# A graph network's nodes retiled: 24 tiles of 128 and one of 53 in place of 25 tiles of 125

## The chip, the cores and the metric

The kernel runs on one core of one Trainium2 chip. The metric is the device time of one execution in microseconds, the median of several.

## The reference

There are 3125 nodes with 128 features and 53125 directed edges (with one loop per node), sorted by destination. First comes a graph network of 12 steps on `h = relu(layernorm(x))`, added to x, then two graph convolutions on the layer norm of the sum:

```python
h = tanh(h @ W_in + b_in)
for _ in range(12):
    agg  = segment_sum(h[src], dst) / deg
    diff = tanh(gelu(agg @ W1 + b1) @ W2 + b2)      # 128 -> 256 -> 128
    h    = h + (diff - decay * h) * 0.5
x = x + h
h = relu(layernorm(x))
h = relu(gcn_conv(h, G1, gb1)); x = x + gcn_conv(h, G2, gb2)
# gcn_conv: segment_sum((h @ W)[src] * dinv[src] * dinv[dst], dst) + b, with another loop per node
```

## The kernel before

**Layout.** Nodes lie in 25 tiles (`TILES`) of 125 (`P`): node `k * 125 + p` is row p of tile k. `state` is [125, 25, 128] in float32. The float32 values are split into two float16 parts, `hi` and `lo`, scaled by a power of two. The edges become a dense count matrix `adj` [125 source rows, 25 source tiles, 3125 destinations] in float16, kept in SBUF, so that a sum over edges is a matrix product.

**Edge sums.** `edge_sums` (lines 550 to 569) makes the sums for one of seven groups of destinations, `GROUPS`: six of four tiles (500 columns) and the tail of one (125 columns). For each source tile k it streams `adj[:, k, columns]` twice into one PSUM bank: against the stationary tile `hi[:, k, :]` (L566) and against `lo[:, k, :]` (L567). A turn is all seven groups; there are 12 turns in the loop and 2 in the convolutions. In group 0 TensorE waits for the split of each group of tiles as it comes to it.

**A step.** After the edge sums of group g TensorE makes `outputs(g - 2)` (L587, float32, two passes of 256 hidden rows in halves) and `hidden(g - 1)` (L578, float32, two halves). DVE multiplies by the inverse degrees (`means`, L960), adds the bias (L967), updates the state (L972) and makes `lo` (L800). ScalarE makes gelu (L681), tanh (L689) and `hi` (L637). At the end of a step come `hidden(TAIL)`, `outputs(TAIL - 1)`, `outputs(TAIL)`.

**The start.** SP issues the load of 125 chunk firsts, seven loads of x (L330, one per group), and then the weights, biases and `clearance` (`s_w`, L331 to L342). DVE counts window starts, POOL gathers edges by indirect DMA. DVE waits for `s_w` before its tables (L745 on), makes the first layer norm (L768 to L793), and takes part in the entry product. It then splits each source into tile and row (L842 to L859) while POOL compares destinations (L440, `s_hits`), reduces the hits (L862), and builds one-hot operands (L881) from which TensorE makes `adj` (L505, ScalarE copies it out, L660).

**Degrees.** The norms go out to DRAM and come back, after `adj` is complete, as a row broadcast to 128 partitions (L371) and as a column per node (L374), for DVE at `s_norms_in`. TensorE starts the first step without them.

**Between the loop and the convolutions.** x is loaded again (L393), DVE adds loops to the diagonal of `adj` (L1009, L1012), makes x2 (L1018), statistics and the second split (L1033 to L1037). x2 goes to DRAM (L397) and comes back (L403) under the convolutions. The result is stored in seven DMAs (L410).

A branch for inputs that the windows can't hold (`missed`) isn't taken with these inputs.

Of the kernel before, what the change touches and what calls it, by code (L numbers as in the profile page):

```python
# [20 lines left out]
F32 = mybir.dt.float32  # L21
F16 = mybir.dt.float16
I32 = mybir.dt.int32
ALU = mybir.AluOpType
# [4 lines left out]
P = 125  # L29
TILES = NODES // P  # L30
# [8 lines left out]
GROUPS = [(g * GROUP_TILES, min(GROUP_TILES, TILES - g * GROUP_TILES)) for g in range(7)]  # L39
NG = len(GROUPS)  # L40
TAIL = NG - 1

WIN = 5
WINDOWS = NODES // WIN
WCOLS = WINDOWS // P
SLOTS = 128
CHUNK = EDGES // P
# [11 lines left out]
OPEN = 1  # L59

# [4 lines left out]
def gnn_kernel(nc, x, src, dst, W_in, b_in, W1, b1, W2, b2, clearance, G1, gb1, G2, gb2, out):  # L65
    ctx = ExitStack()
    with ctx:
# [31 lines left out]
        scratch = sb("scratch", [128, 5587], F32)  # L99
# [3 lines left out]
        def col(n):  # L103
# [25 lines left out]
        xload = scratch[0:P, 0:TILES * FEAT].rearrange("p (k f) -> p k f", f=FEAT)  # L129
        o = TILES * FEAT  # L130
        agg = [scratch[:, o:o + 500], scratch[:, o + 500:o + 625]]
        o += 625
        hid = [scratch[:, o:o + 1000].rearrange("p (h n) -> p h n", h=2),
               scratch[:, o + 1000:o + 1250].rearrange("p (h n) -> p h n", h=2)]
        lnt = [scratch[0:P, o:o + 512], scratch[0:P, o + 512:o + 1024]]
        o += 1250
        act_out = scratch[0:P, o:o + 512]
        stats = scratch[0:P, o:o + TILES * 6].rearrange("p (k s) -> p k s", s=6)
        ones_row = scratch[0:1, o - 225:o - 97]
        assert o + 512 == 5587  # L140

        half = scratch[:, :].bitcast(F16)
        nl, nr = 128 * BATCH, P * BATCH
# [10 lines left out]
        assert o <= 5587 * 2  # L154

        yT = [scratch[:, 768 + 500 * i:1268 + 500 * i] for i in range(2)]
        etanh = [scratch[0:P, 1768 + 512 * i:2280 + 512 * i] for i in range(2)]

        o = 0
        e_dst = scratch[0:P, o:o + CHUNK]  # L160
        e_src = scratch[0:P, o + CHUNK:o + 2 * CHUNK]
        o += 2 * CHUNK
        e_sk = scratch[0:P, o:o + CHUNK]
        e_raw = scratch[0:P, o + CHUNK:o + 2 * CHUNK]
        o += 2 * CHUNK
        h = 2 * o
        c625 = half[0:P, h:h + BLOCK]
        h += BLOCK + 1
        gL = half[0:P, h:h + SUB * 128].rearrange("p (c i) -> p c i", c=SUB)
        h += SUB * 128  # L170
        gR = half[0:P, h:h + SUB * BLOCK].rearrange("p (c i) -> p c i", c=SUB)
        h += SUB * BLOCK + 1
        g_one = half[0:P, h:h + 128]
        g_zero = half[0:P, h + 128:h + 256]
        h += 256
        g_rest = half[0:P, h:h + BLOCK]
        h += BLOCK + 1
        g_deg = scratch[0:1, h // 2:h // 2 + BLOCK]
        assert h // 2 + BLOCK <= 5587


        room = adj_flat[:, :].bitcast(F32)
        roomi = adj_flat[:, :].bitcast(I32)
# [23 lines left out]
        wsrc = place(n)  # L207
        quot_i = place(n, roomi)
        quot = place(n)
# [91 lines left out]
        c_use = [sem(f"gcn{n}_rows_ready") for n in range(2)]  # L301
        s_diag = sem("loops_added")
# [6 lines left out]
        x_v = x.rearrange("(k p) f -> p k f", p=P)  # L309
        out_v = out.rearrange("(k p) f -> p k f", p=P)  # L310
        x2_v = x2_dram.rearrange("(k p) f -> p k f", p=P)
# [5 lines left out]
        def window_layout(a):  # L317
            return a.rearrange("(g q d) -> q g d", g=WCOLS, q=P)
# [3 lines left out]
        def _(sp):  # L322
# [24 lines left out]
            with sp.If(missed != 0):  # L347
# [3 lines left out]
                with sp.Fori(0, 5) as j:  # L351
                    with sp.Fori(0, TILES) as k:
# [8 lines left out]
                sp.dma_start(deg[0:P, :].rearrange("p (g d) -> p g d", g=WCOLS), window_layout(deg_dram)  # L361
                             ).then_inc(g_degl, 16)

            sp.wait_ge(s_norms, 1)
            sp.dma_start(window_layout(rdeg_dram), rdeg[0:P, :].rearrange("p (g d) -> p g d", g=WCOLS)
                         ).then_inc(s_norms_out, 16)
            sp.dma_start(window_layout(dinv_dram), dinv[0:P, :].rearrange("p (g d) -> p g d", g=WCOLS)
                         ).then_inc(s_norms_out, 16)
            sp.wait_ge(s_norms_out, 32)
            sp.wait_ge(s_last[2], 1)  # L370
            sp.dma_start(row, rdeg_dram.rearrange("(a n) -> a n", a=1).broadcast_to((128, NODES))  # L371
                         ).then_inc(s_norms_in, 16)
            with nc.allow_non_contiguous_dma("a column of one float per node"):
                sp.dma_start(dinv_col[0:P, :], dinv_dram.rearrange("(k p) -> p k", p=P)).then_inc(s_norms_in, 16)  # L374


            def stream_rest(turn, g):
                k0, nt = GROUPS[g]
                with sp.Fori(0, TILES) as k:
                    sp.wait_ge(s_restu, (turn * NG + g) * TILES + k + OPEN)  # L380
                    sp.dma_start(rest_tile[:, 0:nt * P],
                                 rest_dram[bass.ds(k, 1), :, k0 * P:(k0 + nt) * P].rearrange("k p d -> p (k d)")
                                 ).then_inc(s_rest[g], 16)
# [7 lines left out]
            for g in range(NG):  # L391
                k0, nt = GROUPS[g]
                sp.dma_start(xload[:, k0:k0 + nt, :], x_v[:, k0:k0 + nt, :]).then_inc(s_xr[g], 16)  # L393
# [3 lines left out]
            sp.dma_start(x2_v, state[:, :, :]).then_inc(s_x2o, 16)  # L397
# [3 lines left out]
            sp.wait_ge(s_x2o, 16)  # L401
            sp.wait_ge(c_lo[1], NG)
            sp.dma_start(state[:, :, :], x2_v).then_inc(s_x2i, 16)  # L403
# [3 lines left out]
            for g in range(NG):  # L407
                k0, nt = GROUPS[g]
# [720 lines left out]
```

## Time and profile before

| | us |
|---|---|
| median of 3 runs | 1447.96 (1447.82 to 1449.18) |
| profiled execution | 1448.8 |
| its span, first to last instruction | 1447.0 |
| TensorE busy | 1305.8 (90%) |
| DVE busy | 427.1 (30%) |
| ScalarE busy | 311.8 (22%) |
| mean granted TensorE clock | 0.977 |

Busy times overlap between engines, and a matmul's recorded duration includes its way through the array, so the distance from start to start is its cost in a stream. L with a number is a line of the kernel above; SPq is SP's instruction queue, PEld the weight loads.

### The profile page before, as it was taken

Reading aid. Unit: us, or ns where it says so; the run is one execution under the profiler, and the core shown is the slowest. Engines: PE = TensorE matmul, PEld = TensorE weight load, DVE = VectorE, ACT = ScalarE, POOL = GpSimd, SP = SyncE. Lnnn points to the kernel's source line nnn. Section 1 sums busy time; section 2 is a strip of 40 time slices with the busy share of each in tenths; the row PEclk is TensorE's granted clock in tenths of the full one; section 3 lists DMA queues with packets and bytes.
Section 4 is the critical chain, followed back from the end, with each engine's and each line's share of the span. In section 5 each row is a group of like instructions: output and inputs, shape, how many; then the busy total and the mean of one; then the engine's idle time right before and its main releaser. Section 6 shows DMA issues by size and latency. Waiting matters only on the chain.

```text
span 1447.0 us, 17636 instructions
## 1 busy us (share of the span) xinstructions
PE 1305.8 (90%) x7256; PEld 731.2 (51%) x7256; DVE 427.1 (30%) x802; ACT 311.8 (22%) x429; POOL 31.5 (2%) x31
## 2 busy tenths in 40 slices
PE   0348899999999999999999999999999999849898
PEld 0337745546455554555545555455554555515444
DVE  1999911301213022131121312113121131382312
ACT  0238821301212012121121212112121131300100
POOL 2320000000000000000000000000000000000000
PEclk9969999999999999999999999999999999969999
DMA  3000020000000000000000000000000000130021
GB/s 94 19 0 0 0 46 1 1 0 0 0 0 0 0 0 0 0 0 0 0 0 0 0 0 0 0 0 0 0 0 0 0 0 0 32 102 1 9 51 31
DMA packets 23951, 13.93 MB, mean 10 GB/s; under 512 B 6358, under 2 KB 23326, under 8 KB 23676
## 3 DMA queue, kind: packets, MB, share of 16 engines
q1 hardware_dynamic: 22332, 11.96, 3.2%
q0 software_dynamic: 1600, 1.72, 0.5%
q8 instruction: 12, 0.20, 0.1%
q14 instruction: 7, 0.06, 0.0%
HBM read 10.43 MB, written 3.23 MB: 9 GB/s over the span
## 4 chain that ended last, share of the span: by engine, by line
PE 82%; DVE 10%; issue 4%; SPq 2%; ACT 1%; DMA 0%; DVEq 0%; ACTq 0%
PE ps L566 32%; PE ps L567 32%; PE ps L587 9%; PE ps L578 8%; DVE scratch L881 3%; SPq L330 1%; ACT scratch L681 1%; PE ps L612 1%; DVE scratch L768 1%; DVE ps L967 1%; DVE state L793 1%; DVE lo L800 0%; DVE scratch L1033 0%; PE ps L476 0%; DMA cols<-in_L_gnn_clearance_dram 0%
## 5 line engine op out<-in xcount | busy, mean ns | idle before, releaser
L566 PE MATMUL ps<-adj,hi 125*128 125x500 f16 (+1 forms) x2450 | 828.4, 353 | 29.9 <-DVE lo L1037 25.3
L567 PE MATMUL ps<-adj,lo 125*128 125x500 f16 (+1 forms) x2450 | 827.0, 352 | 0.0
L566 PEld LDWEIGHTS ps<-adj,hi 125*128 125x128 f16 x2450 | 237.6, 97 | 281.8 <-issue 43.7
L567 PEld LDWEIGHTS ps<-adj,lo 125*128 125x128 f16 x2450 | 238.3, 97 | 253.2 <-issue 22.4
L967 DVE TENSOR_TENSOR ps<-ps,bias 125x512 f32<-125x512 f32 (+1 forms) x84 | 53.8, 640 | 561.6 <-PE ps L587 561.6
L689 ACT ACTIVATE scratch<-ps 125x512 f32<-125x512 f32 (+1 forms) x84 | 46.3, 552 | 669.3 <-DVE ps L967 669.3
L578 PE MATMUL ps<-scratch,w 128*128 128x500 f32 (+1 forms) x336 | 141.1, 542 | 13.7 <-ACT scratch L681 13.7
L681 ACT ACTIVATE scratch<-ps,b1c,cols 128x500 f32<-128x500 f32 (+1 forms) x168 | 113.5, 723 | 156.8 <-PE ps L578 156.0
L587 PEld LDWEIGHTS ps<-w,scratch 128*125 128x125 f32 x1200 | 140.5, 188 | 6.6
L587 PE MATMUL ps<-w,scratch 128*125 128x128 f32 x1200 | 143.5, 273 | 0.0
L960 DVE TENSOR_TENSOR scratch<-ps,scratch 128x500 f32<-128x500 f32 (+1 forms) x84 | 52.0, 619 | 188.7 <-PE ps L578 129.9
L505 PE MATMUL ps<-scratch 128*128 128x125 f16 x625 | 81.7, 297 | 16.1 <-DVE scratch L881 15.9
L881 DVE TENSOR_TENSOR scratch<-scratch 128x1536 f16<-128x1536 f16 (+1 forms) x106 | 93.0, 937 | 1.7 <-DVE scratch L870 0.4
L660 ACT ACTIVATE adj<-ps 125x1500 f32 x52 | 77.3, 1486 | 38.6 <-PE ps L505 38.6
L578 PEld LDWEIGHTS ps<-scratch,w 128*128 128x128 f32 x336 | 56.3, 190 | 58.0 <-issue 33.0
L505 PEld LDWEIGHTS ps<-scratch 128*128 128x128 f16 x625 | 66.7, 120 | 30.8 <-DVE scratch L881 30.7
L972 DVE SCALAR_TENSOR_TENSOR state<-state,cols,scratch 125x512 f32<-125x512 f32 (+1 forms) x84 | 58.4, 696 | 58.6 <-ACT scratch L689 58.6
L800 DVE SCALAR_TENSOR_TENSOR lo<-state,cols,hi 125x512 f16<-125x512 f32 (+1 forms) x91 | 58.7, 690 | 33.7 <-ACT hi L637 33.7
L637 ACT ACTIVATE hi<-state,cols 125x512 f16<-125x512 f32 (+1 forms) x91 | 55.8, 666 | 0.1
L467 PE MATMUL ps<-ident,state 125*128 125x125 f32 x25 | 5.0, 340 | 43.8 <-DVE state L793 43.8
L1048 DVE TENSOR_TENSOR scratch<-ps,scratch 128x500 f32<-128x500 f32 (+1 forms) x14 | 8.7, 623 | 105.3 <-PE ps L612 94.1
L467 PEld LDWEIGHTS ps<-ident,state 125*128 125x128 f32 x25 | 3.9, 179 | 43.9 <-issue 43.9
(115 smaller groups left out, 228.0 us busy)
## 6 DMA issues: line engine op xcount, KB each, us to landing
scratch<-rdeg_scratch SPq DMA_DIRECT2D x1, 1562.5 KB
scratch<-dinv_scratch SPq DMA_DIRECT2D x1, 1562.5 KB, 6.7
x_scratch<-state SPq DMA_DIRECT2D x1, 1562.5 KB
state<-x_scratch SPq DMA_DIRECT2D x1, 1562.5 KB
state<-in_x_dram SPq DMA_DIRECT2D x6, 250.0 KB
scratch<-in_x_dram SPq DMA_DIRECT2D x6, 250.0 KB
out_dram<-state SPq DMA_DIRECT2D x6, 250.0 KB
w<-in_L_gnn_W_dram SPq DMA_DIRECT2D x2, 128.0 KB
```

The lines of the kernel that those rows point to most:

```text
L505: return nc.tensor.matmul(target[:, :, place * WIN:(place + 1) * WIN], Lb[buf][:, b, :, i_], Rb[buf][:, b, :, i_].rearrange("p (k d) -> p ...
L566: nc.tensor.matmul(bank, hi[:, k, :], adj[:, k, c0:c0 + n], start=(k == 0), stop=False)
L567: mm = nc.tensor.matmul(bank, lo[:, k, :], adj[:, k, c0:c0 + n], start=False, stop=(k == TILES - 1))
L578: nc.tensor.matmul(ps_hid[h][:, 0:n], w1[:, h * FEAT:(h + 1) * FEAT], agg[g == TAIL][:, 0:n], start=True, stop=True).then_inc(s_hid, 1)
L587: mm = nc.tensor.matmul(ps_out[g == TAIL][0:P, i * FEAT:(i + 1) * FEAT], hid[g == TAIL][:, h, i * P:(i + 1) * P], w2[:, h, :], start=(h == ...
L637: nc.scalar.activation(tiles_of(hi, group), tiles_of(state, group), ACT.Copy, scale=factor).then_inc(s_hi, 1)
L660: nc.scalar.activation(adj[:, :, bass.ds((i * 2 + u) * BATCH * WIN, BATCH * WIN)].rearrange("p k (b c) -> p b k c", b=BANKS), ps[0:P, 3 * ...
L681: nc.scalar.activation(hid[g == TAIL][:, h, 0:n], ps_hid[h][:, 0:n], ACT.Gelu, bias=b1c[:, h:h + 1], scale=now_unscale).then_inc(s_gelu, 1)
L800: V.scalar_tensor_tensor(out=tiles_of(lo, group), in0=tiles_of(state, group), scalar=factor, in1=tiles_of(hi, group), op0=ALU.mult, op1=AL ...
L881: last_ = V.tensor_tensor(buf[:, 0:b, :, 0:w], c_.broadcast_to((128, b, m, w)), k_.broadcast_to((128, b, m, w)), ALU.is_equal)
L967: V.tensor_tensor(p_, p_, bias_of(1, nt), ALU.add).then_inc(s_bias, 1)
L972: V.scalar_tensor_tensor(out=tiles_of(state, g), in0=tiles_of(state, g), scalar=keep[0:P, :], in1=act_out[:, 0:n_], op0=ALU.mult, op1=ALU. ...
```

## The change

Tiles have 128 rows, so 3125 nodes are 24 full tiles (`FULL`) and one of 53 (`SHORT`, tile 24). Its `hi` is in rows 0 to 63 of the stationary tile and its `lo` in rows 64 to 127 (`STACK`), padded with zeros; the rows of `adj` for that tile are copied by a DMA from partitions 0 to 63 to 64 to 127 (`s_pair`). One matmul per group serves both parts. The groups cover 512 columns five times, then 437 (tiles 21 to 23 and the short one), then 128 (tile 20, the tail). Source tiles are taken in `K_ORDER`: 0 to 19, 21 to 23, 24, 20, and in group 0 there is a wait in front of each.

```diff
-P = 125
-TILES = NODES // P
+P = 128
+FULL = NODES // P
+LAST = NODES - FULL * P
+TILES = FULL + 1
+SHORT = TILES - 1
+STACK = 64
...
+GROUPS = [(0, 4), (4, 4), (8, 4), (12, 4), (16, 4), (21, 4), (20, 1)]
+SPANS = [(k0 * P, min(nt * P, NODES - k0 * P)) for k0, nt in GROUPS]
+K_ORDER = [(k, g) for g, (k0, nt) in enumerate(GROUPS[:TAIL]) for k in range(k0, k0 + nt) if k != SHORT]
+K_ORDER += [(SHORT, TAIL - 1), (GROUPS[TAIL][0], TAIL)]
...
             def edge_sums(turn, g, split, first):
-                k0, nt = GROUPS[g]
-                c0, n = k0 * P, nt * P
+                c0, n = SPANS[g]
...
-                for k in range(TILES):
-                    if g == 0 and k % GROUP_TILES == 0:
-                        pe.wait_ge(split, first + k // GROUP_TILES + 1)
+                for at, (k, owner) in enumerate(K_ORDER):
+                    if g == 0:
+                        pe.wait_ge(split, first + owner + 1)
+                        if k == SHORT:
+                            pe.wait_ge(s_pair, 16)
...
+                    nc.tensor.matmul(bank, hi[:, k, :], adj[:, k, c0:c0 + n], start=(at == 0), stop=False)
+                    if k != SHORT:
+                        mm = nc.tensor.matmul(bank, lo[:, k, :], adj[:, k, c0:c0 + n], start=False,
+                                              stop=(k == K_ORDER[-1][0]))
```

`hidden`, `gelu`, `means` and `scaled` take their columns from `SPANS`; `outputs`, `tanh`, bias and update work on whole tiles (512 columns in group 5, cleared once beyond 437). The split on DVE writes the short tile's `lo` with an instruction of its own, in the loop, in the second layer norm and before the second convolution:

```diff
+            def lo_of(group, values, factor):
+                k0, nt = GROUPS[group]
+                k1 = min(k0 + nt, FULL)
+                if k1 < k0 + nt:
+                    V.scalar_tensor_tensor(out=hi[STACK:P, SHORT, :], in0=values[0:STACK, SHORT, :],
+                                           scalar=factor[0:STACK, :],
+                                           in1=hi[0:STACK, SHORT, :], op0=ALU.mult, op1=ALU.subtract)
+                return V.scalar_tensor_tensor(out=lo[:, k0:k1, :], in0=values[:, k0:k1, :], scalar=factor,
+                                              in1=hi[:, k0:k1, :], op0=ALU.mult, op1=ALU.subtract)
```

Loads and stores of nodes go through `rows`, which gives a group's full tiles as one DMA and the 53 rows as another, so eight DMAs for all nodes. Store and reload of x2, single DMAs before, go the same way. The loads of x wait for a POOL memset of the short tile, POOL's first instruction:

```diff
+        def rows(t, dram, g):
+            k0, nt = GROUPS[g]
+            k1 = min(k0 + nt, FULL)
+            pairs = [(t[:, k0:k1, :], dram[k0 * P:k1 * P, :].rearrange("(k p) f -> p k f", p=P))]
+            if k0 + nt == TILES:
+                pairs.append((t[0:LAST, SHORT, :], dram[FULL * P:NODES, :]))
+            return pairs
...
+            sp.wait_ge(s_pad, 1)
             for g in range(NG):
-                k0, nt = GROUPS[g]
-                sp.dma_start(state[:, k0:k0 + nt, :], x_v[:, k0:k0 + nt, :]).then_inc(s_x[g], 16)
+                for sbuf, dram in rows(state, x, g):
+                    sp.dma_start(sbuf, dram).then_inc(s_x[g], 16)
...
             sp.wait_ge(s_last[2], 1)
+            sp.dma_start(adj[STACK:P, SHORT, :], adj[0:STACK, SHORT, :]).then_inc(s_pair, 16)
             sp.dma_start(row, rdeg_dram.rearrange("(a n) -> a n", a=1).broadcast_to((128, NODES))
                          ).then_inc(s_norms_in, 16)
...
-                sp.dma_start(dinv_col[0:P, :], dinv_dram.rearrange("(k p) -> p k", p=P)).then_inc(s_norms_in, 16)
+                sp.dma_start(dinv_col[:, 0:FULL], dinv_dram[0:FULL * P].rearrange("(k p) -> p k", p=P)
+                             ).then_inc(s_norms_in, 16)
+                sp.dma_start(dinv_col[0:LAST, SHORT:TILES], dinv_dram[FULL * P:NODES].rearrange("(k p) -> p k", p=LAST)
+                             ).then_inc(s_norms_in, 16)
```

Windows of edges keep their layout (125 windows a column). The split of a source into tile and row is now two integer operations; fourteen DVE instructions become eight, and the copy ahead of `s_wd` is gone:

```diff
-            V.tensor_copy(wsrc, wsrc_i.rearrange(flat))
             V.tensor_tensor(wdst, wdst_i, base, ALU.subtract).then_inc(s_wd, 1)
-            dve.wait_ge(s_wd, 1)
+            e_ = wsrc_i.rearrange(flat)
+            V.tensor_scalar(rem_i, e_, P - 1, None, ALU.bitwise_and)
+            link(V.tensor_scalar(quot_i, e_, 7, None, ALU.logical_shift_right))
```

Also added: on DVE a second corner of the diagonal, a piece of x2 and two memsets before the loop; on POOL two small memsets.

## Rows read from the trace of the kernel before

**Rows 1.** The page: busy time, chain by engine, and a group of weight loads.
```profile
PE 1305.8 (90%) x7256; PEld 731.2 (51%) x7256; DVE 427.1 (30%) x802; ACT 311.8 (22%) x429; POOL 31.5 (2%) x31
...
PE 82%; DVE 10%; issue 4%; SPq 2%; ACT 1%; DMA 0%; DVEq 0%; ACTq 0%
...
L566 PEld LDWEIGHTS ps<-adj,hi 125*128 125x128 f16 x2450 | 237.6, 97 | 281.8 <-issue 43.7
```

**Rows 2.** Timeline of the last groups: start us, duration us, engine, line.
```profile
1424.64 0.37 PE L567 MATMUL ps<-adj,lo 125*128 125x500 f16 x1
...
1434.80 0.37 PE L567 MATMUL ps<-adj,lo 125*128 125x500 f16 x1
...
1435.88 0.22 PE L566 MATMUL ps<-adj,hi 125*128 125x125 f16 x1
...
1437.99 0.22 PE L566 MATMUL ps<-adj,hi 125*128 125x125 f16 x1
```

**Rows 3.** The chain of waits in step 11: start us, us, what.
```profile
1157.42 1.75 PE ps L587 x16
1159.17 1.68 PE ps L578 x4
```

**Rows 4.** Timeline from the end of step 11 into step 12.
```profile
1166.76 1.42 ACT L681 ACTIVATE scratch<-ps,b1c,cols 128x500 f32<-128x500 f32 x2
...
1168.24 0.71 PE L578 MATMUL ps<-scratch,w 128*128 128x125 f32 x4 [1.14 <-ACT scratch L681]
...
1168.76 0.80 ACT L681 ACTIVATE scratch<-ps,b1c,cols 128x125 f32<-128x125 f32 x2 [0.58 <-PE ps L578]
...
1172.58 0.38 PE L567 MATMUL ps<-adj,lo 125*128 125x500 f16 x1
...
1172.79 0.37 PE L566 MATMUL ps<-adj,hi 125*128 125x500 f16 x1
...
1176.95 1.01 DVE L800 SCALAR_TENSOR_TENSOR lo<-state,cols,hi 125x512 f16<-125x512 f32 x2 [0.26 <-ACT hi L637]
```

**Rows 5.** Timeline of the start, SP's queue, POOL and DVE.
```profile
1.29 19.88 SPq L330 DMA_DIRECT2D state<-in_x_dram  x7
...
12.41 1.21 POOL L429 DMA_INDIRECT adj<-in_dst_dram,adj  x1 [0.30 <-issue]
21.22 0.83 SPq L331 DMA_DIRECT2D w_in<-in_L_gnn_W_in_dram  x1
...
31.77 0.15 DVE L745 TENSOR_SCALAR cols<-cols 128x1 f32<-128x1 f32 x1 [25.95 <-DMA cols<-in_L_gnn_clearance_dram]
```

**Rows 6.** Windows: length, busy by engine, clock granted, DMA share, GB/s.
```profile
21.40:22.40 1.00, 0.00 (x0) 0.00 (x0) 0.00 (x0) 0.00 (x0) 0.00 (x0) 1.00 0.38 95
...
23.40:24.40 1.00, 0.00 (x0) 0.00 (x0) 0.00 (x0) 0.00 (x0) 0.00 (x0) 1.00 0.97 255
...
186.00:196.00 10.00, 8.36 (x32) 3.55 (x33) 0.32 (x1) 2.81 (x4) 0.00 (x0) 0.83 0.11 3
...
200.00:202.00 2.00, 2.00 (x11) 0.87 (x9) 0.00 (x0) 0.00 (x0) 0.00 (x0) 1.00 0.99 404
```

**Rows 7.** Timeline of the window keys, DVE and POOL.
```profile
71.67 0.48 DVE L842 CAST adj<-adj 125x640 f32<-125x640 int32 x1
...
72.98 10.31 POOL L440 TENSOR_SCALAR adj<-adj 125x640 f32<-125x640 f32 x5 [18.07 <-DVE adj L843]
...
83.56 3.47 DVE L862 TENSOR_REDUCE cols<-adj 125x25 f32<-125x3200 f32 x1
```

**Rows 8.** Timeline of the first step's start.
```profile
187.64 0.37 PE L566 MATMUL ps<-adj,hi 125*128 125x500 f16 x1 [2.05 <-ACT adj L666]
...
196.25 0.35 SPq L371 DMA_DIRECT2D scratch<-rdeg_scratch  x1
```

**Rows 9.** Who waited for whom: total us, times, longest.
```profile
PE ps L566 <- DVE lo L1037: 25.3, 3, 24.6
```

**Rows 10.** The same for SP's queue.
```profile
SPq L67 <- DMA out_dram<-state: 4.3, 1, 4.3
```

More of the change, by code:

```diff
@@ L59 @@
 OPEN = 1
+SCRATCH = TILES * FEAT + 512 + 128 + 1024 + 256 + 512
 SPLIT_TOP = 14
@@ L301, in gnn_kernel @@
         c_use = [sem(f"gcn{n}_rows_ready") for n in range(2)]
+        s_pad = sem("short_tile_cleared")
+        s_pair = sem("short_tile_paired")
+        g_pair = sem("general_rest_paired")
         s_diag = sem("loops_added")
@@ L308, in gnn_kernel, with parts @@
         block = ctx.enter_context(nc.Block())
-        x_v = x.rearrange("(k p) f -> p k f", p=P)
-        out_v = out.rearrange("(k p) f -> p k f", p=P)
-        x2_v = x2_dram.rearrange("(k p) f -> p k f", p=P)
+        def rows(t, dram, g):
[5 more added lines that the diff above has]
+            return pairs
+        def parts(g):
+            return 2 if sum(GROUPS[g]) == TILES else 1
         def tiles_of(t, g):
@@ L391, in _ @@
             for g in range(NG):
-                k0, nt = GROUPS[g]
-                sp.dma_start(xload[:, k0:k0 + nt, :], x_v[:, k0:k0 + nt, :]).then_inc(s_xr[g], 16)
+                for sbuf, dram in rows(xload, x, g):
+                    sp.dma_start(sbuf, dram).then_inc(s_xr[g], 16)
             sp.wait_ge(s_x2, NG)
@@ L396, in _ @@
                          ).then_inc(s_dinv, 16)
-            sp.dma_start(x2_v, state[:, :, :]).then_inc(s_x2o, 16)
+            for g in range(NG):
+                for sbuf, dram in rows(state, x2_dram, g):
+                    sp.dma_start(dram, sbuf).then_inc(s_x2o, 16)
             with sp.If(missed != 0):
@@ L400, in _ @@
                     stream_rest(STEPS, g)
-            sp.wait_ge(s_x2o, 16)
+            sp.wait_ge(s_x2o, 16 * (NG + 1))
             sp.wait_ge(c_lo[1], NG)
-            sp.dma_start(state[:, :, :], x2_v).then_inc(s_x2i, 16)
+            for g in range(NG):
+                for sbuf, dram in rows(state, x2_dram, g):
+                    sp.dma_start(sbuf, dram).then_inc(s_x2i, 16)
             with sp.If(missed != 0):
@@ L407, in _ @@
             for g in range(NG):
-                k0, nt = GROUPS[g]
                 sp.wait_ge(c_use[1], g + 1)
-                sp.dma_start(out_v[:, k0:k0 + nt, :], state[:, k0:k0 + nt, :]).then_inc(s_res, 16)
-            sp.wait_ge(s_res, 16 * NG)
+                for sbuf, dram in rows(state, out, g):
+                    sp.dma_start(dram, sbuf).then_inc(s_res, 16)
+            sp.wait_ge(s_res, 16 * (NG + 1))
         @block.gpsimd
@@ L760, in _, with statistics @@
             V.tensor_scalar(unscale, pow2, 2.0**-SPLIT_TOP * DT, None, ALU.mult).then_inc(s_tab, 1)
-            mv = mean_var[0:P, :].rearrange("p (k s) -> p k s", s=2)
-            def statistics(rows):
-                for k in range(TILES):
-                    if k % GROUP_TILES == 0:
-                        rows(k // GROUP_TILES)
-                    last = V.bn_stats(stats[:, k, :], state[:, k, :])
+            mv = mean_var[:, :].rearrange("p (k s) -> p k s", s=2)
+            def statistics(ready):
+                for g, (k0, nt) in enumerate(GROUPS):
+                    ready(g)
+                    for k in range(k0, k0 + nt):
+                        last = V.bn_stats(stats[:, k, :], state[:, k, :])
                 link(last)
@@ L853, in _ @@
[L853 removed]
+            V.tensor_scalar(rem, rem_i, 1.0, None, ALU.add)
             V.tensor_scalar(over, w_, 0.0, None, ALU.is_ge)
[L856 removed]
+            link(V.scalar_tensor_tensor(out=keyf, in0=quot_i, scalar=float(WIN), in1=w_, op0=ALU.mult, op1=ALU.add))
             link(V.scalar_tensor_tensor(out=inside, in0=w_, scalar=float(WIN), in1=over, op0=ALU.is_lt, op1=ALU.mult))
[L858 removed]
@@ L1048, in scaled @@
                     V.tensor_tensor(agg[g == TAIL][:, 0:n_], ps_agg[2 if g == TAIL else g % 2][:, 0:n_],
-                                    row[:, k0 * P:k0 * P + n_], ALU.mult).then_inc(c_aggT[layer], 1)
+                                    row[:, c0:c0 + n_], ALU.mult).then_inc(c_aggT[layer], 1)
                 def rows_out(g):
```

273 lines of the change are left out of this document (139 added, 134 removed).

## The prediction

> **What bounds the kernel now.** I read the page first, then the chain of waits, then the timeline of three places: one step of the loop, the start, and the end. Timeline durations of matmuls overlap, so I take a matmul's cost from the distance between starts.
>
> The page says TensorE is busy 90% of the span, and 82% of the chain that ended last runs through it [rows 1]. So inside the loop a saved TensorE cycle is a saved cycle. What else lies on the chain is a short list: DVE 10%, which is mostly the start, SP's queue 2%, and ScalarE 1%.
>
> The unit of work is `edge_sums`. Its matmuls of 500 columns start every 211.7 ns (from 1424.64 to 1434.80 us, 48 steps) and those of 125 columns every 55.5 ns (from 1435.88 to 1437.99, 38 steps) [rows 2]. That gives 0.4165 ns for a column and 3.4 ns for the instruction. The pace is set by columns streamed, not by weight loads: a load of 97 ns [rows 1] goes by unseen even behind matmuls 55.5 ns apart.
>
> At the end of a step there is one real stall: TensorE waits 1.14 us for the gelu of group 5 before it may write the tail's hidden product [rows 4]. The splits `hi` and `lo` for the next step arrive in time.
>
> The start is another matter. DVE sits until 31.77 us for the last of the weights, and that load is last because SP's queue spends 19.88 us, from 1.29 us on, on issuing seven loads of x [rows 5]. While only these run, the DMA engines are 0.38 busy and move 95 GB/s. Two microseconds later, with the 128-partition weight loads, they are 0.97 busy and move 255 GB/s [rows 6]. So the 125-partition loads use a part of the engines only, and the queue backs up into SP. After that DVE's own chain runs without a pause to 83.56 us, and everything behind it shifts with it.
>
> **The change, part by part.** The working is against the span of 1447.0 us. The profiled execution took 1448.8, 0.8 above the median of 1447.96, so I take the sum off the median.
>
> *Edge sums.* A turn was 50 matmuls in each of seven groups: 50 x (6 x 211.7 + 55.5) ns = 66.3 us. Now it is 49 matmuls, five groups of 512 columns, one of 437, one of 128. By the line above these cost 216.7, 185.4 and 56.7 ns, so 49 x (5 x 216.7 + 185.4 + 56.7) ns = 65.0 us. There are 14 turns (12 steps, 2 layers): 14 x 1.33 = 18.7 us saved. Columns in all are the same 3125; what is saved is one pass in fifty. Bounds: 18 (columns alone) to 19.5.
>
> *Hidden products.* Four matmuls of 500 columns take 1.68 us [rows 3], 0.84 ns a column each. Twelve more columns in five groups cost 4 x 12 x 0.84 x 5 = 0.20 us a step, 2.4 us in 12. Group 5 falls to 437 columns, but its saving of 0.21 us only lengthens the stall behind it. What shortens that stall is the gelu: 1.42 us for two of 500 columns against 0.80 for two of 125 [rows 4] is 0.83 ns a column, so 2 x 63 x 0.83 = 0.10 us a step, 1.3 us in 12. Net +1.1 us. The `outputs` and `product` matmuls keep their count and their 128 moving columns. Their stationaries widen from 125 to 128, at most 2.4% of the 1.75 us of sixteen [rows 3], under 0.05 us a group, 3 to 4 us if all of it showed. I take nothing, because the pace fits two passes of 128 moving columns (107 ns) plus the 3.4, and I keep 0 to 4 for the range.
>
> *The waits of group 0.* They were seven a turn and are 26 (one for each tile, and `s_pair`). A wait that is already met shows no price: the matmul at 1172.79 is the ninth of its group, has such a wait in front, and starts 0.21 us after its neighbour, like any other [rows 4]. I take 0; the dear end is under the rivals. Are they met? `lo` of group 5 and the tail is done at 1177.96, 6.9 us into a group that started at 1171.10 (1172.79 less eight spacings). Its first user is the 41st matmul, at 8.7 us. The extra DVE instruction on the short tile's `lo` (about 0.3 us) is covered by that margin. The tail's tile is now last in order, which only helps.
>
> *The loads of x.* Now 24 tiles go from 128 partitions, and 53 rows in a DMA of their own, behind a short POOL memset (`s_pad`). SP issues the 1562 KB row broadcast, 128 partitions wide, in 0.35 us [rows 8]. Eight such issues are 2.8 us in place of 19.9. The rest of the chain, from 21.22 to 31.77, is 10.6 us, so the weights could be in at 1.3 + 2.8 + 10.6 = 14.7. The traffic doesn't allow quite that: the transfers up to 31.8 us are some 3.4 MB (summed over windows like those of [rows 6]), 13.3 us at the best rate seen with 512-byte rows, 255 GB/s, after a start at about 2.5. POOL's indirect loads share the engines, and the 53 rows may sit on few of them. I take 17 us for the end of DVE's wait, a gain of 14.8. Bounds: no gain if the loads pace as before, 17.1 at 14.7. What comes next is not late: the gathered chunk rows that DVE needs 4.4 us later have been asked for by POOL at 13.6 us [rows 5].
>
> The Trainium skill, "DMA: Bandwidth & Descriptors", section "Why a DMA increments its semaphore by 16 and not by 1", says a DMA from SP runs on the largest number of engines up to 16 that divides its outermost dimensions: 5 for 125 rows, 16 for 128, 1 for 53. The trace agrees in kind: 0.38 of sixteen busy is near five and their bookkeeping. By it alone the x loads would shrink from 625 to 192 packets an engine (245 on the one that has the 53 rows), some 8 us at the pace of the rows, and the sum would be the one I use.
>
> *Window keys.* Six of DVE's fourteen operations from 71.67 us [rows 7] go, 4 to 5 us of work. But POOL's five compares run from 72.98 for 10.31 us, to 83.3, and DVE needs them next [rows 7]. So only the copy that stood ahead of `s_wd` counts, 0.5 us. If POOL ran faster beside an idle DVE it could be up to 4.
>
> *The copy of the short tile (`s_pair`).* It is a DMA of 64 rows, issued where the row broadcast is now, at 196.25, 8.6 us after the first edge matmul at 187.64 [rows 8]. Its user is the 47th matmul: 46 x 0.217 = 10.0 us, plus about 1.6 for the stretch at the lower clock (0.83 granted on average over 186 to 196 [rows 6]), 11.6 us. It moves 0.4 MB; at the 404 GB/s of large rows [rows 6] that is 1 us, and it has some 3 us. I take a stall of 0.3 us, bounds 0 to 2. The row broadcast behind it is late by 1 us. DVE needs it only for `means(0)`, and TensorE that only after group 1.
>
> *Second layer norm, stores.* TensorE waits 24.6 us there for the first `lo` [rows 9], a chain of DVE work. Added: one piece of `x2`, one corner of the diagonal, one piece of `lo`: +0.3 us. The x reload, the store of `x2` and its reload lie under DVE or edge sums and get shorter. At the very end SP waits 4.3 us for the last store [rows 10], which queues behind group 5's. That shrinks with more engines, while the 53 rows add some 1.7 us on theirs: 1.2 us saved, bounds 0 to 2.
>
> Sum: -18.7 + 1.1 + 0 - 14.8 - 0.5 + 0.3 + 0.3 - 1.2 = -33.5. 1448.0 - 33.5 = 1414.5.
>
> **The rivals.**
> *The x loads are no faster.* If 512-byte rows are what costs and not their spread, SP is blocked as before. For it: all x loads have them. Against it: the weights at 23.4 us are mostly 512-byte rows too and fill the engines [rows 6]. Time: 1414.5 + 14.8 + 1.2 = 1430.5.
>
> *They are faster, but the start is bound elsewhere*, by the gathers or by a single engine that has the 53 rows and its share of everything. Then half the gain comes: about 1422.
>
> *The waits cost (the other side).* If a wait in front of each tile keeps the next weight load from being fetched early, its 97 ns [rows 1] come into the open. 19 more waits in 14 turns are 266; at 97 ns they cost 25.8 us, giving 1440. From 126 ns each (33.5 / 266) they eat the whole gain and the kernel gets slower. Against it: the wait at 1172.79 costs nothing.
>
> *The saved matmul saves nothing*, since wider moving operands cost more than the line says. The line has two points, 125 and 500, and 512 is next to the second: hardly possible. It would leave about 1433.
>
> **How the numbers follow.** Forecast 0.71; loads no faster 0.11; start bound elsewhere 0.10; waits cost 0.06 (of which 0.04 slower than before and 0.01 the same); no saving by the matmul 0.02. The likeliest case alone is 1409 to 1420 (upper bound of the loads' gain, POOL's speed-up in part; stationaries, pair stall and clock on the other side). The range takes in the two cases behind it: 1409 to 1431. A difference within 0.2% (2.9 us) is about what a measurement of this kernel can't tell from none; only a wait price near 126 ns lands there. Faster 0.95, same 0.01, slower 0.04.
>
> **What the profile after should show.** SP's x issues short, and DVE's first wait over near 17 us. A step shorter by 1.24 us (18.7 / 14 less 1.1 / 12), matmuls of 512 columns 216.7 ns apart, and no gap between the tiles of group 0. POOL's compares ended last before DVE's reduction. `s_pair` met within a microsecond. The second layer norm's gap stays near 25 us. The prediction is wrong if the first wait ends after 25 us, or if group 0's matmuls are further apart than group 1's.

## The result and the profile after

The changed kernel takes 1422.22 us, the median of 4 runs (1421.82 to 1422.75), against 1447.89 (1447.57 to 1449.18) for the kernel before, in the same session. The ratio is 0.9821, with a 95% interval of 0.9804 to 0.9838. The forecast was 1414.5 with a range of 1409 to 1431: the direction and the range hold, and the time is 7.7 us above the forecast. The profiled execution took 1421.82 us, its span 1420.0.

First the page of the changed kernel, the lines that answer to [rows 1]: instructions, busy time of each engine, and the matmuls of the fp16 product.

```profile
span 1420.0 us, 17490 instructions
...
PE 1289.5 (91%) x7158; PEld 727.4 (51%) x7158; DVE 426.4 (30%) x815; ACT 311.5 (22%) x429; POOL 31.6 (2%) x34
...
L600 PEld LDWEIGHTS ps<-adj,hi 128*128 128x128 f16 x2450 | 238.3, 97 | 281.8 <-issue 47.4
L602 PEld LDWEIGHTS ps<-adj,lo 128*128 128x128 f16 x2352 | 229.4, 98 | 243.6 <-issue 23.5
```

There are 98 fewer matmuls (14 turns of seven groups, one each), and the `lo` line has 2352 where the `hi` line has 2450: that is the shared tile. A weight load still takes 97 ns. TensorE's busy time fell by 16.3 us and the span by 27.0, so more than a third of the gain is not in the matmuls. The page's chain for this execution covers only some 12% of the span, so I compare the two kernels by landmarks, the starts of one instruction that both have.

The start of the changed kernel, in the timeline view (start us, duration us, engine, line, then in brackets the idle time before and what ended it), answers to [rows 5].

```profile
1.31 4.59 SPq L350 DMA_DIRECT2D state<-in_x_dram  x8
...
5.94 0.43 SPq L351 DMA_DIRECT2D w_in<-in_L_gnn_W_in_dram  x1
...
11.42 1.95 SPq L362 DMA_DIRECT2D cols<-in_L_gnn_clearance_dram  x1
12.55 1.21 POOL L462 DMA_INDIRECT adj<-in_dst_dram,adj  x1 [0.30 <-issue]
20.24 0.15 DVE L780 TENSOR_SCALAR cols<-cols 128x1 f32<-128x1 f32 x1 [14.27 <-DMA cols<-in_L_gnn_clearance_dram]
```

SP is through with eight loads of x in 4.59 us where seven took 19.88, and DVE starts at 20.24 instead of 31.77. But the first weight is issued 15.3 us earlier (5.94 against 21.22) and DVE starts only 11.5 us earlier: what remains of the wait is the time from the last issue (11.42) to its landing.

The window keys and the first step of the changed kernel, same view, answer to [rows 7, 8].

```profile
61.13 10.09 POOL L473 TENSOR_SCALAR adj<-adj 125x640 f32<-125x640 f32 x5 [17.75 <-DVE adj L886]
71.25 3.48 DVE L899 TENSOR_REDUCE cols<-adj 125x25 f32<-125x3200 f32 x1 [4.08 <-POOL adj L473]
...
175.31 0.59 PE L600 MATMUL ps<-adj,hi 128*128 128x512 f16 x1 [2.06 <-ACT adj L701]
...
183.95 0.53 SPq L393 DMA_DIRECT2D adj<-adj  x1
184.52 0.58 SPq L394 DMA_DIRECT2D scratch<-rdeg_scratch  x1
...
186.49 5.53 SPq L399 DMA_DIRECT2D cols<-dinv_scratch  x1
188.04 0.90 PE L600 MATMUL ps<-adj,hi 128*128 128x512 f16 x2 [1.19 <-DMA adj<-adj]
```

DVE now has nothing to do before POOL's compares end, and waits 4.08 us for them. The copy of the short tile is issued 8.64 us after the first edge matmul, as in the forecast, but it holds TensorE up by 1.19 us.

One step of the loop is the distance between two loads of ScalarE's table, from the timeline of ScalarE. Step 2 and step 12 of the changed kernel:

```profile
274.35 1.28 ACT L716 ACT_TABLE_LOAD   x1 [1.67 <-DVE cols L1022]
...
1156.01 1.28 ACT L716 ACT_TABLE_LOAD   x1 [1.67 <-DVE cols L1022]
```

and of the kernel before:

```profile
286.13 1.28 ACT L681 ACT_TABLE_LOAD   x1 [1.45 <-DVE cols L983]
...
1178.65 1.28 ACT L681 ACT_TABLE_LOAD   x1 [1.45 <-DVE cols L983]
```

Ten steps took 892.52 us and take 881.66: 89.25 and 88.17 us a step, 1.09 saved where the forecast had 1.24.

Who waited for whom in the changed kernel (total us, times, longest) answers to [rows 9, 10], and to the stall in [rows 4].

```profile
PE ps L600 <- DVE lo L1089: 25.1, 1, 25.1
...
PE ps L613 <- ACT scratch L716: 14.9, 12, 1.2
...
SPq L77 <- DMA out_dram<-state: 2.7, 1, 2.7
```

The wait at the second layer norm grew from 24.6 to 25.1, the stall for the gelu from 1.14 to 1.24 a step, and the last store is waited for 2.7 us instead of 4.3.

### The profile page after: what moved, and what is told of

Read it like the earlier page. It is cut to its first block and busy times, and to the rows that moved or that the text cites. A ratio compares the mean times of both kernels' runs of the same rounds, so it can differ in the third digit from the quotient of the medians.

```text
span 1420.0 us, 17490 instructions
## 1 busy us (share of the span) xinstructions
PE 1289.5 (91%) x7158; PEld 727.4 (51%) x7158; DVE 426.4 (30%) x815; ACT 311.5 (22%) x429; POOL 31.6 (2%) x34
## 5 line engine op out<-in xcount | busy, mean ns | idle before, releaser
L600 PE MATMUL ps<-adj,hi 128*128 128x512 f16 (+2 forms) x2450 | 815.4, 353 | 31.1 <-DVE lo L1089 25.1
L602 PE MATMUL ps<-adj,lo 128*128 128x512 f16 (+2 forms) x2352 | 796.7, 353 | 0.0
L600 PEld LDWEIGHTS ps<-adj,hi 128*128 128x128 f16 x2450 | 238.3, 97 | 281.8 <-issue 47.4
L602 PEld LDWEIGHTS ps<-adj,lo 128*128 128x128 f16 x2352 | 229.4, 98 | 243.6 <-issue 23.5
L613 PE MATMUL ps<-scratch,w 128*128 128x512 f32 (+2 forms) x336 | 141.0, 542 | 14.9 <-ACT scratch L716 14.9
L716 ACT ACTIVATE scratch<-ps,b1c,cols 128x512 f32<-128x512 f32 (+2 forms) x168 | 113.2, 721 | 156.8 <-PE ps L613 155.8
L622 PEld LDWEIGHTS ps<-w,scratch 128*128 128x128 f32 x1200 | 143.3, 192 | 6.3
L622 PE MATMUL ps<-w,scratch 128*128 128x128 f32 x1200 | 146.1, 275 | 0.0
L695 ACT ACTIVATE adj<-ps 128x1500 f32 x52 | 77.3, 1486 | 38.0 <-PE ps L538 38.0
L840 DVE SCALAR_TENSOR_TENSOR lo<-state,cols,hi 128x512 f16<-128x512 f32 (+2 forms) x98 | 61.2, 671 | 30.6 <-ACT hi L672 29.5
```

Of the source, the lines that this page charges most:

```text
L600: nc.tensor.matmul(bank, hi[:, k, :], adj[:, k, c0:c0 + n], start=(at == 0), stop=False)
L602: mm = nc.tensor.matmul(bank, lo[:, k, :], adj[:, k, c0:c0 + n], start=False, stop=(k == K_ORDER[-1][0]))
L613: nc.tensor.matmul(ps_hid[h][:, 0:n], w1[:, h * FEAT:(h + 1) * FEAT], agg[g == TAIL][:, 0:n], start=True, stop=True).then_inc(s_hid, 1)
L622: mm = nc.tensor.matmul(ps_out[g == TAIL][:, i * FEAT:(i + 1) * FEAT], hid[g == TAIL][:, h, i * P:(i + 1) * P], w2[:, h, :], start=(h == 0 ...
L695: nc.scalar.activation(adj[:, :, bass.ds((i * 2 + u) * BATCH * WIN, BATCH * WIN)].rearrange("p k (b c) -> p b k c", b=BANKS), ps[:, 3 * u: ...
L716: nc.scalar.activation(hid[g == TAIL][:, h, 0:n], ps_hid[h][:, 0:n], ACT.Gelu, bias=b1c[:, h:h + 1], scale=now_unscale).then_inc(s_gelu, 1)
```

## The experiments

Every kernel below is the changed kernel with the one edit shown ("..." marks lines left out). The ratio is against the kernel before, run on the same chip beside it; a distance in us from "the changed kernel" is from its 1422.22, measured in another session. The kernel before took 1447.89, 1447.81, 1447.08 and 1449.07 us in the four sessions, so a distance of 1 or 2 us between two medians isn't evidence by itself, and for such small effects I go by landmarks inside the traces.

**Is it the width of the x loads?** The eight loads stay where they are, and each full one is cut at partition 125.

```diff
-                    sp.dma_start(sbuf, dram).then_inc(s_x[g], 16)
+                    if sbuf.shape[0] == LAST:
+                        sp.dma_start(sbuf, dram).then_inc(s_x[g], 16)
+                    else:
+                        sp.dma_start(sbuf[0:125], dram[0:125]).then_inc(s_x[g], 16)
+                        sp.dma_start(sbuf[125:128], dram[125:128]).then_inc(s_x[g], 16)
```

(DVE's wait for x counts one more DMA per group.)

> Only the six wide loads of x at the start are cut in two, partitions 0 to 124 and 125 to 127. Theory (the width of 125 is what confined the loads to a part of the DMA engines): SP's issues of x take 15 to 20 us again, DVE's first wait ends near 30 us and the time is 1431 to 1436, 9 to 14 above the changed kernel's 1422. Rival (the loads got faster because tiles or order differ, or for the larger loads behind them): the first wait stays near 20 us and the time at 1422 to 1424.

Measured: 1433.37 us (1432.65 to 1434.47), ratio 0.9903 [0.9886, 0.9919], 11.2 us more than the changed kernel. Its timeline of SP and DVE at the start:

```profile
2.31 0.28 SPq L353 DMA_DIRECT2D state<-in_x_dram  x1
2.63 2.92 SPq L354 DMA_DIRECT2D state<-in_x_dram  x1
...
22.16 0.37 SPq L355 DMA_DIRECT2D w_in<-in_L_gnn_W_in_dram  x1
...
31.07 0.15 DVE L784 TENSOR_SCALAR cols<-cols 128x1 f32<-128x1 f32 x1 [25.10 <-DMA cols<-in_L_gnn_clearance_dram]
```

and its window of 6 to 8 us (length, busy by engine, granted clock, DMA share, GB/s), then the same window of the changed kernel:

```profile
6.00:8.00 2.00, 0.00 (x0) 0.00 (x0) 0.00 (x0) 0.00 (x0) 1.40 (x1) 1.00 0.38 95
```

```profile
6.00:8.00 2.00, 0.00 (x0) 0.00 (x0) 0.00 (x0) 0.00 (x0) 1.41 (x1) 1.00 1.17 308
```

The same bytes in the same 512-byte rows block SP until 22.16 us, and DVE starts at 31.07, as it did before the change (31.77). The wide piece is taken in 0.28 us and SP then stands in the next issue for 2.92; I read this as a queue that is full behind a transfer that few engines serve. The run also has six more loads than the changed kernel, but the kernel before, with seven in all, kept SP about as long (19.88 us). So the width gives the 11 us, and the rival "the x loads are no faster" is out. The Trainium skill, "DMA: Bandwidth & Descriptors", section "Why a DMA increments its semaphore by 16 and not by 1", says that a DMA uses the largest number of engines up to 16 that divides its slowest dimension, so 5 for 125 rows and 16 for 128. This run agrees in kind: 0.38 of sixteen engines busy and 95 GB/s with 125 rows, all busy and 308 GB/s with 128.

**Why 20 us and not 17: the bias broadcasts?** They are four DMAs with one 512-byte packet for each partition, just ahead of the clearance that DVE waits for.

```diff
             for i, b in enumerate((b_in, b2, gb1, gb2)):
-                sp.dma_start(bias[:, i, :], b.rearrange("(a f) -> a f", a=1).broadcast_to((P, FEAT))
-                             ).then_inc(s_w, 16)
+                for p0, np_ in ((0, 125), (125, 3)):
+                    sp.dma_start(bias[p0:p0 + np_, i, :], b.rearrange("(a f) -> a f", a=1).broadcast_to((np_, FEAT))
+                                 ).then_inc(s_w, 16)
```

(the waits on `s_w` go from 16 * 11 to 16 * 15)

> Only the four bias broadcasts are cut in two, 125 and 3 partitions. In the changed kernel their 512-byte packets come at 12 to 15 us and share the engines for long. Theory (sixteen engines that read the same 512 bytes of DRAM at once hinder each other): with five engines the first wait of DVE, which ends at 20.2 us, ends at 17 to 18.5 and the time is 2 to 3 us lower. Rival (what is slow there is the sum of all traffic, POOL's gathers with it): the first wait ends at 20 to 21 and the time is unchanged or up to 1 us higher.

Measured: 1423.07 us (1422.59 to 1424.27), ratio 0.983 [0.9814, 0.9847]; DVE starts at 21.10. That is at the upper edge of this landmark's scatter: in four kernels whose start is untouched (those of `fiftieth`, `few_waits`, `pair_early` and `narrow_out`) it is between 19.48 and 21.04. Narrower broadcasts gain nothing. The run isn't a clean test of their spread over engines, though: SP took 4.39 us over the six pieces where it took 1.38 over three broadcasts, and so issued the clearance at 14.76 instead of 11.42.

**Or POOL's gathers?** They share the engines with the weights (five indirect loads from 6.29 us on). Here POOL doesn't begin them before the weights are in.

```diff
             pool.wait_ge(s_chunk_i, 1)
+            pool.wait_ge(s_w, 16 * 11)
             for g in range(WCOLS):
```

> POOL's first five gathers start only when the weights are in. Theory (the weights come at 20.2 us and not at 15 because the gathers share the DMA engines with them): DVE's first wait ends at 13.5 to 15.5 us; afterwards it waits for the gathers instead, so the time is 1 to 6 us above 1422. Rival (SP's queue or the one engine with the 53 rows is the brake): the first wait still ends at 19 us or later, and the time is 8 us or more above.

Measured: 1422.91 us (1422.3 to 1423.66), ratio 0.9834 [0.9817, 0.985]. Timeline and waits of this kernel:

```profile
15.37 0.15 DVE L781 TENSOR_SCALAR cols<-cols 128x1 f32<-128x1 f32 x1 [9.40 <-DMA cols<-in_L_gnn_clearance_dram]
...
16.39 1.40 POOL L463 DMA_INDIRECT adj<-in_dst_dram,adj  x1 [12.44 <-issue]
```

```profile
DVE adj L814 <- DMA adj<-in_dst_dram,adj: 5.3, 5, 1.3
```

The weights are in 4.9 us sooner, and DVE gives all of it back by waiting 5.3 us for the gathers. So the gathers are what holds up the weights, and both are wanted: putting one whole set behind the other wins nothing. In the changed kernel it isn't a matter of bytes. Its window of 14 to 15 us, with gathers and weights under way, has every engine busy at 76 GB/s, a quarter of the 308 above:

```profile
14.00:15.00 1.00, 0.00 (x0) 0.00 (x0) 0.00 (x0) 0.00 (x0) 0.00 (x0) 1.00 1.01 76
```

What DVE wants first is one float.

**The clearance ahead of x.** Its DMA goes first, with a semaphore of its own; DVE's first wait changes to it, and TensorE's wait for the weights counts one DMA less.

```diff
+            with nc.allow_non_contiguous_dma("one float on every partition"):
+                sp.dma_start(decay, clearance.rearrange("(a f) -> a f", a=1).broadcast_to((128, 1))
+                             ).then_inc(s_clear, 16)
             sp.wait_ge(s_pad, 1)
...
-            dve.wait_ge(s_w, 16 * 11)
+            dve.wait_ge(s_clear, 16)
```

> The load of clearance, the only one of the weights that DVE's tables need, is issued ahead of the loads of x and has a semaphore of its own. If nothing but that wait holds DVE at the start, its tables are done by about 10 us and it next waits for POOL's gathered rows, which end near 19 us in the changed kernel; the gain is the tables' 4.4 us plus what is left of the wait, 5 to 6 us, time 1416 to 1417. Rival (TensorE's wait for the other weights, or the layer norm's wait for x, comes next and takes its place): a gain under 3 us.

Measured: 1415.6 us (1415.18 to 1417.14), ratio 0.9781 [0.9764, 0.9797], 6.6 us less than the changed kernel. In its timeline the wait is gone, and the next late thing is the gathered rows, asked for at the same times as ever:

```profile
15.07 0.66 DVE L814 TENSOR_SCALAR_CACHE_REDUCE adj<-adj 125x425 f32<-125x425 int32 x1 [1.03 <-DMA adj<-in_dst_dram,adj]
...
20.69 0.66 DVE L814 TENSOR_SCALAR_CACHE_REDUCE adj<-adj 125x425 f32<-125x425 int32 x1 [4.96 <-DMA adj<-in_dst_dram,adj]
```

The first edge matmul starts at 170.43 instead of 175.31. These 4.9 us are what the traces show, as forecast (5 to 6); the 6.6 between the medians has about 1.7 more, which no landmark accounts for, and against the kernel before in each session this edit adds 5.8.

**What does the fiftieth matmul cost?** `lo` of the short tile is multiplied again, so that each group has 50 matmuls as before, at the new widths. (That tile of `lo` holds zeros, since its rows lie in `hi`, so they are added for nothing.)

```diff
-                    if k != SHORT:
-                        mm = nc.tensor.matmul(bank, lo[:, k, :], adj[:, k, c0:c0 + n], start=False,
-                                              stop=(k == K_ORDER[-1][0]))
+                    mm = nc.tensor.matmul(bank, lo[:, k, :], adj[:, k, c0:c0 + n], start=False,
+                                          stop=(k == K_ORDER[-1][0]))
```

> Everything as in the changed kernel, but the short tile's matmul against lo is made too (lo of that tile is all zeros), so 50 matmuls a group again, with the new widths. Theory (a matmul costs columns times 0.4165 ns plus 3.4 ns, whatever lies in it): 98 more matmuls of 216.7, 185.4 and 56.7 ns, 14 x (5 x 216.7 + 185.4 + 56.7) ns = 18.5 us, time 1440 to 1441. Rival (part of the matmuls' cost is hidden or the pass is cheaper at the end of a group): 1432 to 1437.

Measured: 1440.35 us (1439.27 to 1441.99), ratio 0.9952 [0.9936, 0.9969]: 18.1 us more than the changed kernel. Its table loads of steps 2 and 12:

```profile
274.81 1.28 ACT L715 ACT_TABLE_LOAD   x1 [1.68 <-DVE cols L1021]
...
1169.74 1.28 ACT L715 ACT_TABLE_LOAD   x1 [1.68 <-DVE cols L1021]
```

89.49 us a step, 1.33 more than without it, which is what the forecast had.

**Do the waits in group 0 cost?** Only the first tile of each owner keeps its wait, so a turn has 7 and the one for `s_pair`, 8 in all, where it had 26.

```diff
-                        pe.wait_ge(split, first + owner + 1)
+                        if at == 0 or owner != K_ORDER[at - 1][1]:
+                            pe.wait_ge(split, first + owner + 1)
```

> In group 0 TensorE waits once for each group of tiles in place of once for each tile; 18 of the 26 waits of a turn go, 252 in all. Theory of the prediction (a wait that is already met costs nothing): the step period stays 88.17 us and the time within 1 us of 1422. Rival (each has a price, up to the 97 ns of a weight load that comes into the open): up to 24 us faster; at 10 ns each 2.5 us faster.

Measured: 1421.78 us (1421.46 to 1422.13), ratio 0.982 [0.9803, 0.9836]. Ten steps of it, 274.93 to 1156.67 us, are 88.17 us each, the same to the hundredth. A wait that is already met is free here.

This run showed something else. In the changed kernel the granted clock falls at the first edge matmuls, and here it doesn't: its windows (length, busy by engine, granted clock, DMA share, GB/s) of 175 to 180 us, and then those of the changed kernel.

```profile
175.00:180.00 5.00, 3.75 (x18) 1.76 (x19) 0.56 (x3) 2.41 (x4) 0.00 (x0) 1.00 0.11 4
```

```profile
175.00:180.00 5.00, 4.69 (x16) 1.80 (x17) 0.56 (x3) 1.49 (x2) 0.00 (x0) 0.68 0.20 5
```

The first matmuls are 0.22 us apart here and 0.43 there, at the lower of the clock's two levels (1.2 GHz): some 1.5 us. It came to nothing, because TensorE then arrives at the short tile's copy earlier and waits longer (this kernel's timeline):

```profile
184.66 0.53 SPq L393 DMA_DIRECT2D adj<-adj  x1
...
188.66 0.87 PE L601 MATMUL ps<-adj,hi 128*128 128x512 f16 x2 [2.30 <-DMA adj<-adj]
```

2.30 us against 1.19. The copy lands some 4 us after its issue at either clock. These 4 us aren't all waiting. Windows of the changed kernel, whose copy is issued at 183.95:

```profile
184.00:185.00 1.00, 1.00 (x7) 0.43 (x5) 0.00 (x0) 0.00 (x0) 0.00 (x0) 1.00 0.00 0
185.00:186.00 1.00, 1.00 (x6) 0.45 (x5) 0.00 (x0) 0.00 (x0) 0.00 (x0) 1.00 0.94 200
186.00:187.00 1.00, 0.86 (x4) 0.19 (x2) 0.00 (x0) 0.00 (x0) 0.00 (x0) 1.00 1.24 200
```

About 1 us passes before any data moves, the 0.4 MB then take 2 us at 200 GB/s, and about 1 us more passes until TensorE is let go. The forecast had the same bytes at 404 GB/s and nothing around them.

**The copy of the short tile issued first.** SP takes it before it waits for `s_norms`, as soon as the last tiles are there.

```diff
+            sp.wait_ge(s_last[2], 1)
+            sp.dma_start(adj[STACK:P, SHORT, :], adj[0:STACK, SHORT, :]).then_inc(s_pair, 16)
             sp.wait_ge(s_norms, 1)
...
             sp.wait_ge(s_last[2], 1)
-            sp.dma_start(adj[STACK:P, SHORT, :], adj[0:STACK, SHORT, :]).then_inc(s_pair, 16)
```

> The copy of the short tile's rows of adj is issued as soon as adj is complete, ahead of the norms on SP's queue and not behind their round trip. Theory (the wait of 1.19 us for it in step 1 is all that it costs): the wait is gone and the time 1.2 us lower. Rival (the norms, which now queue behind it, are late for the first means and TensorE waits for those instead): no change or slower.

Measured: 1420.12 us (1419.54 to 1421.01), ratio 0.9811 [0.9795, 0.9828], 2.1 us less. Timeline of this kernel, the copy and step 2's table load:

```profile
174.76 0.53 SPq L387 DMA_DIRECT2D adj<-adj  x1
...
272.68 1.28 ACT L717 ACT_TABLE_LOAD   x1 [1.67 <-DVE cols L1023]
```

There is no wait for the copy any more. Step 2's landmark is 1.67 us earlier than in the changed kernel, of which 0.24 is there at the first edge matmul (175.07 against 175.31): the copy's own share is 1.4 us. The rest of the 2.1 is within the scatter between sessions.

**The stationaries of `outputs` back to 125 columns.** This kernel leaves out the product for the last 3 nodes of each tile; two memsets on DVE ahead of the loop, not in the cut below, give those PSUM rows a value.

```diff
-                            mm = nc.tensor.matmul(ps_out[g == TAIL][:, i * FEAT:(i + 1) * FEAT],
-                                                  hid[g == TAIL][:, h, i * P:(i + 1) * P], w2[:, h, :],
+                            mm = nc.tensor.matmul(ps_out[g == TAIL][0:125, i * FEAT:(i + 1) * FEAT],
+                                                  hid[g == TAIL][:, h, i * P:i * P + 125], w2[:, h, :],
```

> The step's output products load stationaries of 125 columns again, in place of 128, and so leave the last 3 nodes of each tile without their product (two small memsets on DVE give those PSUM rows a value). Theory (these float32 matmuls go at the pace of their weight loads, so the wider stationary is what made them 112 ns apart in place of 109): 109 ns again, step period 88.17 less 100 x 2.6 ns = 87.9 us, time about 3 us lower, 1419. Rival (the prediction's reading, two passes of 128 moving columns set the pace): 112 ns and 1422 as before.

Measured: 1419.83 us (1418.99 to 1421.24), ratio 0.9809 [0.9792, 0.9825]. By shape, the weight loads of these matmuls (the second number behind the bar is the mean in ns) in this kernel, then in the changed one:

```profile
L622 PEld LDWEIGHTS ps<-w,scratch 128*125 128x125 f32 x1200 | 140.3, 188 | 6.4
```

```profile
L622 PEld LDWEIGHTS ps<-w,scratch 128*128 128x128 f32 x1200 | 143.3, 192 | 6.3
```

and ten steps of this kernel, which are 87.98 us each, 0.19 less than with 128:

```profile
275.07 1.28 ACT L716 ACT_TABLE_LOAD   x1 [1.67 <-DVE cols L1024]
...
1154.91 1.28 ACT L716 ACT_TABLE_LOAD   x1 [1.67 <-DVE cols L1024]
```

12 x 0.19 is 2.3 us, and the medians differ by 2.4 (which across sessions supports it weakly; the step's length is the evidence). The pace of these matmuls is 109 ns with 125 columns in the stationary tile and 112 with 128. It follows the stationary tile's width and not the 128 moving columns, which are the same in both. That it is the load of the weights that paces them, as I expected, fits its records, 188 and 192 ns, but isn't shown apart from the width.

**All that pays, together.** The clearance first, the copy first, and two of POOL's five compares moved to DVE, which stood idle for them.

```diff
-            for d in range(WIN):
+            for d in range(WIN - 2):
                 last = nc.gpsimd.tensor_scalar(hits[:, :, d, :], wdst, float(d), None, ALU.is_equal)
...
+            for d in (WIN - 2, WIN - 1):
+                last = V.tensor_scalar(hits[:, :, d, :], wdst, float(d), None, ALU.is_equal)
+            link(last)
```

> The changed kernel with three edits: clearance loaded first, the short tile's copy issued early, and two of POOL's five compares of destinations given to DVE, which sat idle for 4.1 us behind them. If the gains lie one behind another on the chain they add up: 6.6 us from the first edit and 2.1 from the second as measured, and about 2 from the third (POOL's three compares take 6.1 us, DVE's keys and two compares some 8.5 from the same start, against 10.1), so 1411 to 1412. Rival (the third moves the wait to TensorE or slows POOL by the shared work): 1413 to 1414.

Measured: 1411.57 us (1410.7 to 1412.62, 5 runs), ratio 0.9747 [0.9733, 0.9761]; the kernel before took 1449.07 beside it. It is the best version of this study, 37.5 us under the kernel before beside it, where the change by itself is 25.7 under the one beside it. POOL and DVE in its timeline, and the first edge matmul:

```profile
55.00 6.45 POOL L475 TENSOR_SCALAR adj<-adj 125x640 f32<-125x640 f32 x3 [17.64 <-DVE adj L888]
...
62.53 3.49 DVE L904 TENSOR_REDUCE cols<-adj 125x25 f32<-125x3200 f32 x1
...
166.68 0.38 PE L602 MATMUL ps<-adj,hi 128*128 128x512 f16 x1 [2.05 <-ACT adj L703]
```

The reduction waits for nobody, and comes 8.7 us before that of the changed kernel. 4.8 of these are already there with the clearance alone first (its reduction starts at 66.41). The sum came out as expected, but with some luck in this execution, whose clock stayed up at the first edge matmuls:

```profile
166.68:171.68 5.00, 5.00 (x24) 2.26 (x25) 0.56 (x3) 1.18 (x2) 0.00 (x0) 1.00 0.58 85
```

Here no wait for the copy stands behind them to take the 1.5 us back. The table load of step 2 comes 11.7 us earlier than in the changed kernel: 8.6 by the first edge matmul, about 1.5 by the copy and about 1.5 by the clock.

## Why the prediction was right, and where 7.7 us went

By the landmarks of the two profiled executions, each stage against its term:

| Stage | Landmark, before and after | Forecast | Measured |
|---|---|---|---|
| End of DVE's first wait | 31.77, 20.24 | -14.8 | -11.5 |
| From there to the reduction | 83.56, 71.25 | -0.5 | -0.8 |
| From there to the first edge matmul | 187.64, 175.31 | 0 | 0.0 |
| Loop and short tile's copy | 1267.13, 1243.40 | -14.6 | -11.4 |
| Second layer norm | 1284.94, 1261.59 | +0.3 | +0.4 |
| Two layers | 1438.82, 1413.23 | -2.7 | -2.2 |
| End of the span | 1447.0, 1420.0 | -1.2 | -1.4 |
| Sum | | -33.5 | -27.0 |

The landmark of the loop's end is DVE's first operation of the second layer norm, and that of the layers is the last `product`. The forecast of the loop is 12 x 1.33 less 1.1 for the hidden products less 0.3 for the copy. The sum misses by 6.5 us. The medians differ by 25.7 us and not by 27.0, since the profiled execution of before was 0.9 above its median and that of after 0.4 below: that is the rest of the 7.7.

*Edge sums* were right, in place and in size: 1.33 us a step by the run with the fiftieth matmul, 1.33 in the forecast. The matmuls of 512 columns are 216.7 ns apart, as the line through 125 and 500 columns gave.

*The x loads* were right in kind and 3.3 us short. The step that failed is the estimate of 17 us for the end of the wait. It counted all bytes at the best rate seen, 13.3 us from 2.5 on, and added 1.2 us for the gathers and the 53 rows; with the gathers held back the wait ends at 15.37, with them at 20.24. That the gathers delay the weights is shown. Why by this much, with the engines 1.01 busy at 76 GB/s, is open. The landmark itself scatters by 1.6 us between kernels with the same start.

*The waits of group 0* were right at 0: 18 fewer of them a turn leave the step at 88.17 us.

*Hidden products* fit: the stall for the gelu grew by 0.10 us a step, the forecast had 0.11 (0.21 longer, 0.10 shorter).

*Outputs.* The term of 0 for the wider stationaries was mis-sized; it is 0.19 us a step, 2.3 in the loop. The forecast read the spacing as two passes of 128 moving columns plus a few ns, which fitted 109 ns by chance. The run with 125 columns shows that the stationary tile's width sets it. The two layers have such products too and miss by 0.4 us; that theirs is the same cause was not tried. These 2.3 us and the copy's 0.9 add up to the loop's 3.2, but they don't match place by place. The ten steps from table load to table load fell 1.5 us short of the forecast, where 0.19 a step makes 1.9. The stretch from the first edge matmul to step 2's table load, 98.49 us before and 99.04 after, fell some 1.5 short, where the copy and one step's outputs make 1.1. About 0.4 us each way stays open.

*The short tile's copy* was right in place and too cheap. The time of issue (8.6 us after the first edge matmul) and of need (11.6) held. The copy was put at 1 us by its bytes and landed 4 us after its issue, 2 of them at half the rate assumed and 2 before and after the data, so the stall was 1.19 where 0.3 was forecast, inside its bounds of 0 to 2. When TensorE runs at the higher clock there, it waits 2.30, so the clock's gain is lost in the wait.

*Window keys*, the *second layer norm* and the *stores* hold within 0.3 us each, with POOL as the last to end before the reduction, as forecast.

The rival that came nearest is "faster, but the start is bound elsewhere, by the gathers", with 1422. Its mechanism is real, but it has 3.3 us of the 7.7 only: 3.2 came from the two terms that were put too low and 1.2 from the executions that were profiled. That the time landed on 1422 is chance. "The loads are no faster", "the waits cost" and "the saved matmul saves nothing" are each shown to be false by a run.

## What to carry to other kernels

When an engine stands at a wait that counts many transfers, ask which of them it needs for its next instruction, and give that one its own semaphore and the first place in the queue; here one float was worth 5 us by the traces. Where an edit widens a tile, cost the stationary side of every small fp32 matmul too, not only the moving columns. A small copy can be late by more than its bytes (here 4 us where they made 1): take the time from issue to landing of a like one from the profile, and issue it before whatever waits in the same queue.

## What the runs showed that I had not expected

The pace of the fp32 matmuls of 128 moving columns (the profile shows two passes for each, and I give the distance between passes) went from 109 to 112 ns when only their stationary tile grew from 125 to 128 columns, whereas fp16 weight loads of 97 ns go by unseen behind matmuls 55.5 ns apart [rows 2].

SP spent 5.53 us on issuing one DMA of 53 single elements (at 186.49 us above), right behind two whose data was still moving. It cost nothing here: DVE's wait for it ended at 195.24, 19.9 us after the first edge matmul, and in the kernel before that distance was 19.9 too (207.54). But anything queued behind it on SP would have stood.

The granted clock at the first edge matmuls was 0.68 over 175 to 180 us in the changed kernel and 1.00 in one that differs from it only in waits. TensorE had stood for 2.06 and 2.05 us before. The waits aren't what decides it: the combined kernel has all of them and stayed at 1.00 too, and in the profiled executions of the nine others, the kernel before among them, the clock fell there. What decides it is open.
